# Attention and the last stage as one program per engine, output products moved round the second products, moments behind the sums, last chunk stored tile by tile

## The reference

```python
def attn(x):                                   # 16 heads of 16
    q, k, v = split(x @ qkv_w + qkv_b)
    write_lines = exterior(x_prev @ w1_write, x @ w2_write)      # 6 components a head
    read_lines  = exterior(x @ w1_read, x @ w2_read)
    std_attn = softmax(causal(q @ k.T * scale))
    geo_attn = softmax(causal(read_lines @ (write_lines @ J6).T * inc_scale))
    std_out, geo_out = std_attn @ v, geo_attn @ (x @ geo_w + geo_b)
    gate = mean(sigmoid(x @ gate_w + gate_b), -1)
    return ((1 - gate) * std_out + gate * geo_out) @ out_w + out_b

def ffn(x):                                    # 768 hidden
    return (silu(x @ wg.T) * (x @ wu.T)) @ wd.T      # integer weights / 127

x = layernorm(x + attn(x))
x = layernorm(x + ffn(x))
```

## Time and profile before

| | us |
|---|---|
| median of 3 runs (1659.74 to 1660.84) | 1659.87 |
| the profiled execution itself | 1661.14 |
| span of the profiled execution, first to last instruction | 1659.4 |
| TensorE busy in it | 1593.2 (96%) |
| ScalarE busy | 1197.9 (72%) |
| VectorE busy | 1073.1 (65%) |
| GpSimd busy | 335.2 (20%) |
| from the last product of attention to the first hidden product | 1342.5 to 1358.0 |
| rounds 0 to 7, first hidden product to last second product | 1358.0 to 1651.5 |
| from there to the end | 1651.5 to 1659.4 |

### The profile page before, as it was taken

How to read it: one execution, slowest core, us unless ns; L and a number is a source line. 1 busy time by engine, 2 the same in 40 slices (tenths; PEclk the granted TensorE clock), 3 DMA queues, 4 the chain that set the end, 5 groups by cost and what they waited for, 6 DMA issues and landing times. The chain is left out here.

```text
span 1659.4 us, 32050 instructions
## 1 busy us (share of the span) xinstructions
PE 1593.2 (96%) x11809; PEld 558.4 (34%) x11809; DVE 1073.1 (65%) x2583; ACT 1197.9 (72%) x1409; POOL 335.2 (20%) x479
## 2 busy tenths in 40 slices
PE   8999799999999999999999999999999979999997
PEld 4555122222222222222222222222222235555664
DVE  5888977666767667676776777667677135544333
ACT  2544189999999999999989999999999841112111
POOL 4444312121221202111120211202111313111000
PEclk9999599999999999999999999999999999999999
DMA  5889442212212122121212202122132122222000
GB/s 168 247 254 264 135 137 64 96 42 86 74 43 89 45 66 67 48 91 45 81 48 70 92 29 84 44 66 71 44 105 63 57 89 84 76 76 89 13 13 25
DMA packets 103262, 140.36 MB, mean 85 GB/s; under 512 B 14032, under 2 KB 72208, under 8 KB 101040
## 3 DMA queue, kind: packets, MB, share of 16 engines
q1 hardware_dynamic: 101888, 135.11, 26.2%
q0 software_dynamic: 624, 2.75, 0.5%
q10 hardware_dynamic: 576, 0.28, 0.1%
HBM read 81.96 MB, written 55.61 MB: 83 GB/s over the span
## 5 line engine op out<-in xcount | busy, mean ns | idle before, releaser
L1261 ACT ACTIVATE prob<-ex 128x1024 f32<-128x1024 f32 (+1 forms) x1152 | 1056.2, 977 | 104.6 <-PE ex L1072 87.8
L1285 DVE TENSOR_REDUCE mp<-mx 128x1 f32<-128x512 f32 x768 | 492.9, 686 | 187.5 <-PE mx L1112 187.4
L1172 PE MATMUL pv<-prob,va 128*32 128x512 f32 (+3 forms) x5120 | 588.2, 541 | 1.6 <-POOL prob L1037 0.4
L1037 POOL TENSOR_SCALAR_AFFINE_SELECT prob<-prob 128x256 f32<-128x256 f32 (+1 forms) x384 | 186.3, 485 | 937.2 <-ACT prob L1261 933.2
L1078 PE MATMUL ex<-dq,dk 34*128 34x512 bf16 (+7 forms) x2560 | 335.7, 348 | 8.0 <-ACT prob L1261 2.2
L1282 DVE CUSTOM_DVE_ANT_0 dull<-mx,mask_qk 128x128 f32<-128x128 f32 (+3 forms) x512 | 223.2, 488 | 88.6 <-PE mx L1112 88.5
L1112 PE MATMUL mx<-dk,dq 64*128 64x512 bf16 (+3 forms) x1280 | 227.6, 356 | 11.6 <-DMA dk<-parts_dot 3.8
L1072 PE MATMUL ex<-gq,gk 38*128 38x512 bf16 (+3 forms) x1280 | 219.1, 355 | 0.0
L1072 PEld LDWEIGHTS ex<-gq,gk 38*128 38x128 bf16 x1280 | 56.4, 93 | 406.8 <-ACT prob L1261 364.1
L1622 ACT ACTIVATE sg<-pg 128x512 f32<-128x512 f32 x48 | 28.7, 598 | 219.9 <-PE pg L1562 219.7
L1172 PEld LDWEIGHTS pv<-prob,va 128*32 128x32 f32 x5120 | 108.4, 108 | 232.3 <-issue 186.5
(11 more groups left out here) (114 smaller groups left out, 911.7 us busy)
## 6 DMA issues: line engine op xcount, KB each, us to landing
values<-vn SPq DMA_DIRECT2D x32, 512.0 KB, 3.8
va<-values SPq DMA_DIRECT2D x16, 1024.0 KB, 5.0
raw<-on SPq DMA_DIRECT2D x64, 256.0 KB
parts_dot<-sp SPq DMA_DIRECT2D x32, 384.0 KB, 4.5
dq<-parts_dot SPq DMA_DIRECT2D x192, 64.0 KB, 3.0
dk<-parts_dot SPq DMA_DIRECT2D x192, 64.0 KB, 2.9
parts_geo<-sp SPq DMA_DIRECT2D x16, 288.0 KB, 4.0
gq<-parts_geo SPq DMA_DIRECT2D x192, 24.0 KB
```

Source lines behind the costliest of these rows:

```text
L1037: g.affine_select(out=cut, in_=cut, compare_op=ALU.is_ge, fill=0.0, base=0, pattern=[[0, nb], [1, P]], channel_multiplier=-1).then_inc(mas ...
L1172: last = pe.matmul(pv[blk * VW:(blk + 1) * VW, CH - w:CH], sets[which]["v"][:, kb, blk * VW:(blk + 1) * VW], prob[UNIT_AT[s, j, kind] % NP ...
L1261: act.activation(prob[n % NPROB][:, :].rearrange("p (b c) -> p b c", b=2)[:, :, 0:w], ex[:, n % 2, :].rearrange("p (b c) -> p b c", b=2)[: ...
L1285: return v.tensor_reduce(out=to, in_=source, axis=AX.X, op=ALU.max)
```

## The change

`project`, `attend` and `finish` become one program per engine, in one block opened in `build`; `finish` uses the PSUM tensors of the other two (`pt` and one `po` in `mx`, the other `po` in `pv`, `pg` in `ex`). GpSimd weighs chunk 2 inside the last attention item. In a round TensorE does `hidden(c)`, the transposes of chunk c + 1, two output products of chunk c + 2, the second products of chunk c, and the other two output products of chunk c + 2. VectorE follows: the blend of chunk c + 2 goes behind `ht` 4, the sums in the order of the products, and both moments (chunk c - 1's second, chunk c + 1's first) to the start of the round. The last chunk's second sums, moments, roots, normalising and stores go tile by tile.

```diff
-        attend(nc, parts, values, raw, gates, ident, mask_qk, gate_z, wide,
-               out_w, out_b, wg, wu, wd, weights, sets, fixed, rden, x, late, shared, ex, mx, pv, first)
-        banks.close()
-        finish(nc, x, raw, gates, rden, ident, weights, out, late)
+        second = attend(nc, sem, parts, values, raw, gates, ident, mask_qk, gate_z, wide,
+                        out_w, out_b, wg, wu, wd, weights, sets, fixed, rden, x, late, shared, ex, mx, pv, first)
+        third = finish(nc, sem, x, raw, gates, rden, ident, weights, out, late, ex, mx, pv)
+        block = ctx.enter_context(nc.Block())
+        @block.sync
+        def _(q):
+            second["sync"](q)
+            third["sync"](q)
...
@@ attend, gpsimd, item @@
                             weigh(g, 1, 1, late, g_passed)
                             residual(g, 1, 1, weights["out_b"], late)
+                            g.wait_ge(late["part_ready"], 1)
+                            weigh(g, 2, 0, late, g_passed)
...
-        pt = pb("pt", [P, NK, CH])
-        pg = [pb(f"pg{i}", [P, 2, CH]) for i in range(2)]
-        po = [pb(f"po{i}", [P, CH]) for i in range(2)]
+        pt = mx[:, 0:NK, :]
+        pg = [ex[:, i, :].rearrange("p (b c) -> p b c", b=2) for i in range(2)]
+        po = [mx[:, NK, :], pv[:, :]]
...
@@ finish, sync, behind the rounds @@
-            q.wait_ge(normed[SECOND], NC * TT)
-            q.dma_start(out_v[NC - 1], res[1][:, :, :]).then_inc(res_st[1], 16)
+            for tt in range(TT):
+                q.wait_ge(normed[SECOND], (NC - 1) * TT + tt + 1)
+                q.dma_start(out_v[NC - 1][:, tt, :], res[1][:, tt, :]).then_inc(res_st[1], 16)
...
-        @block.gpsimd
-        def _(g):
-            with g.Fori(1, NC // 2) as k:
+        def gpsimd(g):
+            residual(g, 2, 0, ob, late)
+            weigh(g, 3, 1, late, g_passed)
+            residual(g, 3, 1, ob, late)
+            with g.Fori(2, NC // 2) as k:
...
@@ finish, tensor @@
                     elif second:
                         pe.wait_ge(sums_ready[FIRST], c * TT)
+                        if tt == 1:
+                            pe.wait_ge(late["on_ready"], ITEMS * NQT)
...
+            def out_part(c, par, tts):
+                pe.wait_ge(mix_ready, c + 1)
+                for tt in tts:
+                    if tt >= 2:
+                        pe.wait_ge(sums_ready[SECOND], (c - 2) * TT + tt + 1)
+                    else:
+                        pe.wait_ge(sums_ready[FIRST], (c - 1) * TT + tt + 3)
                     first_product(pe, tt, po[tt % 2][:, 0:D], mix_t[par], wo, late)
...
-            def down(c, tts, has_first):
+            def down(c, tts, has_first, has_mix):
                 pe.wait_ge(ht_ready, (c + 1) * NM)
                 for tt in tts:
                     if tt >= 2:
                         pe.wait_ge(sums_ready[SECOND], c * TT + tt - 1)
+                    elif has_mix:
+                        pe.wait_ge(sums_ready[FIRST], (c + 2) * TT + tt + 1)
                     elif has_first:
...
-            def round_(c, par, head, has_first):
-                if has_first and not head:
-                    out_chunk(c + 1, 1 - par, False, False)
+            def round_(c, par, head, has_first, has_mix):
                 hidden(c, head)
                 if has_first:
                     turn_normed(c + 1, 1 - par, False)
-                down(c, range(TT), has_first)
+                if has_mix:
+                    out_part(c + 2, par, range(2))
+                down(c, range(TT), has_first, has_mix)
+                if has_mix:
+                    out_part(c + 2, par, range(2, TT))
...
@@ finish, vector @@
-            def round_(c, par, has_first, has_mix, has_second, second_head):
+            def round_(c, par, has_first, has_mix, has_second, second_head, first_all=False):
+                if first_all:
+                    totals(c + 1, 1 - par, FIRST, range(TT), False)
+                if has_second:
+                    spread(c - 1, SECOND)
                 if has_first:
-                    add_up(c + 1, 1 - par, FIRST, False)
+                    spread(c + 1, FIRST)
                 for m in range(NM):
...
                     if m == 3 and has_second:
                         normalise(c - 1, 1 - par, SECOND, second_head)
+                    if m == 4 and has_mix:
+                        blend(c + 2, par, False)
                 if has_mix:
-                    blend(c + 2, par, False)
-                add_up(c, par, SECOND, not has_second)
+                    totals(c + 2, par, FIRST, range(2), False)
+                if has_first:
+                    totals(c, par, SECOND, range(TT), not has_second)
+                if has_mix:
+                    totals(c + 2, par, FIRST, range(2, TT), None)
...
-            scales(NC + 2, 1, 2)
-            normalise(NC - 1, 1, SECOND, False)
+            v.wait_ge(res_st[1], (NC // 2 - 1) * 16)
+            for tt in range(TT + 1):
+                if tt < TT:
+                    last_total(tt)
+                if tt:
+                    last_rows(tt - 1)
```

More of the change, by code:

```diff
@@ L262, in build @@
             "den": sb("den", [P, CH]), "den_gate": sb("den_gate", [P, CH]),
-            "on": [sb(f"on{i}", [P, CH]) for i in range(2)],
+            "on": [sb(f"on{i}", [P, CH]) for i in range(2)], "on_ready": sem("on_ready"),
             "sums": sb("sums0", [P, TT, D]), "stat": sb("stat", [P, 2, TT, 6]),
@@ L272, in build, with _ @@
             "mv_ready": [sem(f"mv_ready{i}") for i in range(2)], "var_ready": [sem(f"var_ready{i}") for i in range(2)]}
-        attend(nc, parts, values, raw, gates, ident, mask_qk, gate_z, wide,
-               out_w, out_b, wg, wu, wd, weights, sets, fixed, rden, x, late, shared, ex, mx, pv, first)
-        banks.close()
-        finish(nc, x, raw, gates, rden, ident, weights, out, late)
+        second = attend(nc, sem, parts, values, raw, gates, ident, mask_qk, gate_z, wide,
[6 more added lines that the diff above has]
+            third["sync"](q)
+        @block.gpsimd
+        def _(g):
+            second["gpsimd"](g)
+            third["gpsimd"](g)
+        @block.tensor
+        def _(pe):
+            second["tensor"](pe)
+            third["tensor"](pe)
+        @block.scalar
+        def _(act):
+            second["scalar"](act)
+            third["scalar"](act)
+        @block.vector
+        def _(v):
+            second["vector"](v)
+            third["vector"](v)
 def operand_set(sb, sem, i):
@@ L874, in attend @@
         pv_done = sem("pv_done")
-        on_ready = sem("on_ready")
+        on_ready = late["on_ready"]
         mx_ready = sem("mx_ready")
@@ L1424, in _, with finish @@
             take(ITEMS - 1, NQT - 1, False)
-def finish(nc, x, raw, gates, rden, ident, weights, out, late):
+        return {"sync": sync, "gpsimd": gpsimd, "tensor": tensor, "scalar": scalar, "vector": vector}
+def finish(nc, sem, x, raw, gates, rden, ident, weights, out, late, ex, mx, pv):
     NT = NC * TT
@@ L1634, in _, with vector @@
             round_(NC - 1, False, False)
-            roots(None, NC)
-        @block.vector
-        def _(v):
+            for tt in range(TT):
+                act.wait_ge(var_ready[SECOND], NC + tt)
+                act.activation(std[:, SECOND, tt:tt + 1], var_eps[:, SECOND, tt:tt + 1], ACT.Sqrt)\
+                   .then_inc(std_ready, 1)
+        def vector(v):
             def blend(c, par, head):
@@ L1646, in blend, with totals @@
                 mixed(v, par, late)
-            def add_up(c, par, norm, head):
-                if not head:
+            def totals(c, par, norm, tts, head):
+                if head is False:
                     v.wait_ge(normed[norm], c * TT)
-                for tt in range(TT):
+                for tt in tts:
                     if norm == FIRST:
```

79 lines of the change are left out of this document (42 added, 37 removed).

## The result

| | before | after |
|---|---|---|
| median of the runs, us | 1660.15 (4 runs) | 1643.64 (4 runs, 1642.77 to 1644.09) |
| ratio | | 0.9894, 95% interval 0.9883 to 0.9906 |
| span of the profiled execution | 1659.4 | 1641.0 |
| last product of attention to T(0), from start to start | 16.38 | 7.61 |
| round 0, T(0) to T(1) | 37.79 | 39.58 |

The forecast was 1641 us, with a range of 1633 to 1649. Of the 18.4 us between the two profiled spans 8.8 come from the seam, 7.3 from rounds 1 to 6, 3.3 from the end, and 0.8 from attention, which the change does not touch: its last products begin at 1340.85 where they began at 1341.66. Round 0 lost 1.8. That share of attention is noise. In the twelve profiled executions of this study, with programs that are the same up to there but for small insertions, those products begin between 1339.88 and 1343.55.

The account below looks back on a forecast made before the run. TensorE's waits in the seam behind attention and in the rounds were taken as removable; 8.7 + 7.9 + 2.4 = 19.0 us off the 1659.4 span gives 1640.4, median 1641 us, range 1633 to 1649.

Parts of the forecast that it names:

- Part 1: Seam between attention and last stage: one program removes the block's end and the pause behind it; 8.7 us won.
- Part 2: Rounds: two output products go ahead of the second products, covering the `ht` wait; 35.5 us a round, 2.25 less.
- thin cover: Rounds: first sum ends 23.1 us after T, second products need it at 23.2; VectorE 0.5 late costs 0.4.
- Round 0: T(0) to T(1): 36.2 us in place of 37.8, the first sum needing chunk 2's residual at 1372.7.
- Part 3: Start of rounds 1 to 4: GpSimd's weighing holds VectorE's `var_eps`; 6.4 us given back, 2.5 + 3 x 1.3.
- Part 4: Kernel's end, last chunk tile by tile: 2.0 us won in the chain to the last result, 0.4 in the store.
- No holding: Rival, rounds: operands land earlier or later, so `var_eps` falls outside the weighing; 6.4 us less, 1634.5; chance 0.20.
- the seam stays: Rival, seam: another engine waits there or TensorE's half speed stays until T(0); half the seam gain lost, 1645; chance 0.08.
- it does nothing: Rival, rounds: second products wait for sums as before for `ht`; only seam and end won, 1649; chance 0.04.
- More holding: Rival, rounds: both sets of moments held; 3 us in each of four rounds, 0.4 in five, 1649; chance 0.15.
- The slower one: Rival, end of attention: chunk 2's operands land after GpSimd's masks; one us per us beyond 1334, decisive from 1353; chance 0.03.

Follow-up runs that it names:

- the kernel that has this part alone: Kernel before with one program per engine, shared PSUM and chunk 2's weighing in the last attention item, rounds and last chunk in old order; median 1652.73 us, ratio 0.9944.
- The kernel with the pause filled: Changed kernel with five products of unread result on TensorE between round 0's first output products and second products; 1639.42 us in one execution.
- the early load: Changed kernel with the load of `x` of chunk 2 issued in front of the wait for attention's last store; median 1640.64 us, ratio 0.9880.
- the second profile: The changed kernel again, without an edit; median 1644.66 us, ratio 0.9895.
- Two kernels that take the meeting away, from either side: Changed kernel with epsilon in ScalarE's root, no `var_eps` step: 1635.88 us; changed kernel with GpSimd's weighing of chunks 4 to 7 awaiting the sixth `ht`: 1635.58 us.
- the kernel with both losses taken away: Changed kernel with epsilon in ScalarE's root and the load of `x` of chunk 2 issued before the wait for attention's last store; median 1633.49 us, ratio 0.9834.

## Why the prediction was right or wrong, point by point

**Part 1 was right.** From the last products to T(0) the forecast had 7.6 us; it was 7.61, and 7.62 in the kernel that has this part alone. The weighing before the masks cost nothing: it ran from 1330.86 to 1335.69, and GpSimd then still waited 0.18 us for ScalarE before the first mask. Chunk 2's operands had landed 3 us before the bound. That the move of one GpSimd step is nearly half of the gain is what the prediction's reading of the held normalising steps implied.

**Part 2 was right for the plain rounds.** Forecast 35.5, measured 35.3 wherever nothing is held. The thin cover between the first sum and the second products, forecast at 0.1 us, held in all of them: no second product of rounds 1 to 5 waited for a sum.

**Round 0 was wrong in sign.** Forecast 36.2 us, 1.6 less than before; it was 39.58, 1.8 more. The step that failed is "the second products start at 1373.2 and T(1) is 1373.2 + 10.46 + 1.83". First, the wait: `x` of chunk 2 landed 12.2 us behind its issue in place of 11.5, the residual ended at 1373.5 where 1372.7 was forecast, and T(0) was 0.8 earlier by attention, so the pause was 2.25 us and not some 0.7 (36.2 less 35.5). Second, the clock: the prediction looked for a falling clock in the seam alone, and took the 10.46 us for granted here. It was 12.1: the granted clock stood at 0.55 to 0.59 behind the pause. The kernel with the pause filled shows that part as 1.7 us, the early load shows both as 4.1. Why the clock fell behind this pause and not behind others as long stays open.

**Part 3 was right in mechanism and in sum, not in its shares.** Forecast 6.4 us given back, measured 6.5 from start to start, 6.6 in the second profile. But round 1 was forecast at 2.5 and gave back 1.0, round 2 at 1.3 and gave back 2.5; that these two errors nearly cancel in the sum is luck. The step that was mis-sized is where the weighing begins: in round 1 the load went out 23.8 us after T(0), not 22.3, but T(1) slid 2.5 us later through round 0, so the weighing began 0.28 and not 1.8 to 3.0 after T(1); in round 2 it began 1.78 after T(2). Two kernels that take the meeting away, from either side, lose the whole wait. The trace settles two points that were open. The residual holds `var_eps` as the weighing does: the second `var_eps` takes 0.44 or 0.45 us in each of the four rounds and ends with the residual. And the rule of the Trainium skill (GPSIMD Engine Reference, Key points), that GpSimd contends with VectorE steps that read two SBUF inputs as with those in a two-port mode, agrees with the blends of 4.98 us under the weighing and 3.37 us under the residual; the prediction had no row for them.

**Part 4 was right for the chain, too careful for the store.** From the last product to the last result 2.4 us, forecast 2.5. From there to the end of the span 2.2 us, forecast 3.0 with 2.4 as the lower bound: the stores of 128 KB landed 1.7 us after their issue in the median, those of 512 KB before 2.9.

**The sum.** Against the span, forecast 1640.4 and measured 1641.0. That it came so near is in part luck, since errors cancel: round 0 was forecast 3.4 us too low, the store 0.8, attention 0.8 and the five plain rounds 0.2 each too high. The median stands 2.6 above the span of the profiled execution, where 0.5 was forecast; that execution was the fastest of the four.

**The rivals.** No holding is refuted, and so are "the seam stays" (7.61 us) and "it does nothing". "More holding" gave each of four rounds 3 us; only round 2, whose weighing began at T + 1.78, came near with 2.5, and the others lost 1.0 to 1.6. The slower one needed a landing at 1353, and chunk 2 had landed by 1331. Not tried: whether attention's last store, which holds back all the loads behind it by some 8 us (issued at 1342.56, the next issue at 1350.51), could be awaited later.

## What to carry to other kernels

When steps are put in a new order, look not only for the engine's own time but for what another engine does to it at that place: here a step over four columns took up to 3.8 us in place of 0.17, since it came to stand beside GpSimd, and TensorE lost up to 2.5 us a round by it. Such a meeting can be undone from either side, by giving the step to another engine or by letting GpSimd wait for a harmless stretch, and both were worth 6.5 us. A gain in front of a transfer that did not move turns into a wait, and on TensorE a wait can cost twice, as it did in round 0: once as itself and once as the slow products behind it. So a new wait in front of a stretch of products makes the time of those products uncertain too.

## What the runs showed of the hardware

GpSimd's `tensor_tensor` between SBUF tiles holds a `tensor_scalar` that VectorE begins beside it to its own end: `var_eps` takes up to 4.37 us instead of 0.17, and in the kernel before the first of the four normalising steps takes 3.55 instead of 0.40. It holds a `tensor_tensor` with two SBUF inputs as well, which then ends 1.1 us behind it (the blend, 4.98 instead of 1.22). It leaves alone `bn_stats` (1.40 us either way), `bn_aggr`, and the first sum, one of whose inputs is in PSUM (0.42 us either way). In these rows the instruction that began first was the one not held: the weighing of chunk 3 took 4.95 us beside a blend begun 0.66 us earlier, in the kernel with the early load, where it takes 4.51.

TensorE's granted clock was 0.50 to 0.77, in stretches of two microseconds, behind pauses of 2.25, 2.28, 2.81 and 2.83 us in round 0 of four profiles, and 0.50 behind one of 3.19 in the seam. It stayed at 1.00 behind a pause of 1.40 us at the same place in round 0, and where the pause of some 2.3 us was filled with products. But it stayed at 1.00 too behind 2.33 us in the seam of the kernel before, behind 2.23 us in round 2 of the changed kernel, behind 2.61 us in round 1 of the kernel with the weighing of chunk 2 back behind attention, and behind 3.15 us in round 0 of the kernel with both losses taken away:

```profile
1376.00:1378.00 2.00, 2.00 (x10) 1.64 (x11) 0.94 (x3) 0.00 (x0) 0.75 (x1) 1.00 0.22 44
```

So the length of a pause does not by itself tell whether the clock falls behind it. What else does is not shown.
